# First attention of a two-layer gated network: where the second copy of each head's high half is written

## The reference

```
x = x + tanh(g_xattn[0]) * attention0(layernorm(x), ctx, ctx)
x = x + tanh(g_ffn[0])   * bit_linear_ffn(layernorm(x), ...)
x = x + tanh(g_xattn[1]) * attention1(layernorm(x), ctx, ctx, Wq, Wk, Wv)
x = x + tanh(g_ffn[1])   * experts(layernorm(x), ...)
```

```
scores = einsum('bqnd,bknd->bnqk', qh, kh) * (1 / sqrt(16))
probs  = softmax(scores, axis=-1)
out    = einsum('bnqk,bknd->bqnd', probs, vh)
```

## Time and profile before

| | |
|---|---|
| median of 3 runs | 2035.0 us (2025.68, 2035.0, 2039.9) |
| the profiled execution's own time | 2015.55 us |
| its span, first to last instruction | 2013.8 us |
| mean granted TensorE clock | 0.944 |
| first attention | from 39 to about 350 us, 64 tiles |
| busy shares of the span | PE 81%, PEld 55%, DVE 80%, ACT 59%, POOL 45% |

### The profile page before, as it was taken

The page is one execution under the profiler, slowest core; times in us unless marked ns, Lnnn a source line. Parts: engine busy times, 40 slices in busy tenths (PEclk is TensorE's granted clock), DMA queues, the critical chain, the costliest instruction groups (busy, mean ns, idle before and its releaser), DMA issues. The chain is left out here.

```text
span 2013.8 us, 53124 instructions
## 1 busy us (share of the span) xinstructions
PE 1628.2 (81%) x20058; PEld 1113.8 (55%) x20058; DVE 1620.7 (80%) x2986; ACT 1181.7 (59%) x1912; POOL 901.8 (45%) x930
## 2 busy tenths in 40 slices
PE   1899999266666666638998999997899999999998
PEld 0677777234444444426776666775455555555555
DVE  6899999558889888876887877876778778787785
ACT  1889988287776777616877777876222222222222
POOL 1455555048788778853333333332232332332322
PEclk9999999689988998869999999998899999999999
DMA  9000000100000000000002000000221211212211
GB/s 320 17 1 0 0 0 0 43 0 1 1 0 0 0 0 0 0 16 2 3 2 66 3 3 2 3 2 2 71 79 53 94 63 53 94 63 74 83 52 63
DMA packets 45435, 66.88 MB, mean 33 GB/s; under 512 B 6272, under 2 KB 36736, under 8 KB 45312
## 3 DMA queue, kind: packets, MB, share of 16 engines
q1 hardware_dynamic: 45024, 65.05, 9.7%
q10 hardware_dynamic: 288, 0.00, 0.0%
HBM read 56.39 MB, written 8.65 MB: 32 GB/s over the span
## 5 line engine op out<-in xcount | busy, mean ns | idle before, releaser
L632 ACT ACTIVATE a_exp<-a_score_t 128x1024 f32<-128x1024 f32 x256 | 262.3, 1024 | 113.4 <-PE a_score_t L442 112.6
L1514 POOL TENSOR_TENSOR e_a_parts<-e_act,e_a_parts 128x512 f16<-128x512 f32 x128 | 150.5, 1175 | 377.5 <-ACT e_a_parts L1486 377.5
L557 DVE TENSOR_REDUCE a_maxes<-a_score 128x8 f32<-128x1024 f32 x256 | 311.2, 1216 | 0.5 <-PE a_score L425 0.5
L1486 ACT ACTIVATE e_a_parts<-e_act 128x512 f16<-128x512 f32 x128 | 80.6, 629 | 343.1 <-DVE e_act L1326 343.1
L1071 POOL TENSOR_TENSOR b_hidden<-b_hidden,b_shifted 128x508 f32<-128x508 f32 x128 | 184.9, 1445 | 145.4 <-DVE b_hidden L924 145.4
L1221 PE MATMUL e_out<-e_down_t,e_a_parts 128*128 128x256 f16 x1536 | 188.9, 273 | 18.6 <-POOL e_a_parts L1514 18.6
L1207 PE MATMUL e_up_ps<-e_n_turned,e_up_t 128*128 128x512 f16 x768 | 187.1, 380 | 5.3 <-DVE e_act L1322 5.3
L1078 POOL TENSOR_TENSOR b_hidden<-b_hidden,b_scales 128x512 f32<-128x512 f32 x128 | 188.0, 1472 | 3.1 <-ACT b_scales L1053 3.1
L1207 PE MATMUL e_gate<-e_n_turned,e_gate_t 128*128 128x512 f16 x768 | 187.9, 381 | 0.2 <-issue 0.2
L1221 PEld LDWEIGHTS e_out<-e_down_t,e_a_parts 128*128 128x128 f16 x1536 | 146.6, 98 | 59.7 <-POOL e_a_parts L1514 28.9
L690 POOL TENSOR_TENSOR a_split<-ctx,a_split 128x256 f16<-128x256 f16 (+1 forms) x64 | 42.8, 669 | 305.2 <-ACT a_split L649 305.2
(11 more groups left out here) (204 smaller groups left out, 4047.3 us busy)
## 6 DMA issues: line engine op xcount, KB each, us to landing
ctx<-e_weights SPq DMA_DIRECT2D x64, 512.0 KB, 5.6
out<-x SPq DMA_DIRECT2D x16, 512.0 KB, 2.9
x<-in_x SPq DMA_DIRECT2D x3, 2048.0 KB, 16.9
ctx<-in_ctx SPq DMA_DIRECT2D x1, 4096.0 KB, 26.8
ctx<-in_ctx SPq DMA_DIRECT2D x1, 3072.0 KB, 16.4
b_raw<-in_L_ffn_w SPq DMA_DIRECT2D x2, 1024.0 KB, 7.1
x<-in_x SPq DMA_DIRECT2D x1, 1536.0 KB, 16.4
ctx<-in_ctx SPq DMA_DIRECT2D x1, 1024.0 KB, 13.4
```

Of the source, the lines that this page charges most:

```text
L557: nc.vector.tensor_reduce(maxes[:, p * PAIRS:(p + 1) * PAIRS], score[:, :].rearrange("p (h k) -> p h k", k=P), AX.X, ALU.max).then_inc(max ...
L632: nc.scalar.activation(exp32[:, u % 2, 2 * p:2 * p + 2, :], score_t[:, :].rearrange("p (g n) -> p g n", g=2), ACT.Exp, scale=DH ** -0.5 / ...
L1514: nc.gpsimd.tensor_tensor(a_parts[:, e % 2, 1, :], act3[:, e % 2, :], a_parts[:, e % 2, 0, :], ALU.subtract).then_inc(alo_ok, 1)
```

## The change

On ScalarE, L652 and L667 write the high halves once, into place 0 of each head. GpSimd gets two more instructions in each of the steps 0 to 63: behind the keys' low half a copy of place 0 to place 2, behind the queries' low half a copy of place 0 to place 1. The signals `kl_ok` and `ql_ok` move from the subtraction to the copy behind it.

```diff
-                            nc.scalar.activation(k_stack[:, u % KR, :, 0:3:2, :], twice(m.ctx[:, i, :]), ACT.Copy).then_inc(kh_ok, 1)
+                            nc.scalar.activation(k_stack[:, u % KR, :, 0, :], heads(m.ctx[:, i, :]), ACT.Copy).then_inc(kh_ok, 1)
...
-                        nc.scalar.activation(q_stack[:, u % 2, :, 0:2, :], twice(normed[:, u % 2, :]), ACT.Copy).then_inc(qh_ok, 1)
+                        nc.scalar.activation(q_stack[:, u % 2, :, 0, :], heads(normed[:, u % 2, :]), ACT.Copy).then_inc(qh_ok, 1)
...
                             nc.gpsimd.tensor_tensor(k_stack[:, u % KR, :, 1, :], heads(m.ctx[:, i, :]), k_stack[:, u % KR, :, 0, :],
-                                                    ALU.subtract).then_inc(kl_ok, 1)
+                                                    ALU.subtract)
+                            nc.gpsimd.tensor_copy(k_stack[:, u % KR, :, 2, :], k_stack[:, u % KR, :, 0, :]).then_inc(kl_ok, 1)
...
                             nc.gpsimd.tensor_tensor(q_stack[:, u % 2, :, 2, :], heads(normed[:, u % 2, :]), q_stack[:, u % 2, :, 0, :],
-                                                    ALU.subtract).then_inc(ql_ok, 1)
+                                                    ALU.subtract)
+                            nc.gpsimd.tensor_copy(q_stack[:, u % 2, :, 1, :], q_stack[:, u % 2, :, 0, :]).then_inc(ql_ok, 1)
```

## The result

| | before | with the change |
|---|---|---|
| median, 20 runs each | 2030.82 us | 2042.38 us (2036.05 to 2053.38) |
| ratio, 95% interval | | 1.0068 (1.0050 to 1.0086) |
| profiled execution, span | 2013.8 us | 2039.1 us |
| spacing of L594 in the loop | 4.82 us | 5.13 us |

A forecast was written before the change was run, and what follows sets the result against it. The first attention was taken to be bound by VectorE and TensorE waiting for each other, 4.82 us a step. L694 delaying L602, with smaller terms, adds 18.7 us to 2035.0: 2053.7 us, own range 2045 to 2062, stated range 2036 to 2090.

The forecast's parts named there:

- slower: Whole kernel: median more than 1% above the kernel before; chance 0.48.
- within 1%: Whole kernel: median within 1% (20 us) of the kernel before; chance 0.47.
- The ring: First attention: VectorE (L594 to L582, 2.88 us) and TensorE (1.94) wait for each other, 4.82 us a step; ScalarE hangs aside.
- ScalarE's 0.21 us: L652 and L667 write 256 elements, not 512: each saves 0.21 us, and L694 begins 0.10 ahead of L602.
- The collision: First attention: L694 on GpSimd holds up L602 on VectorE, 0.31 us more a step, 0.40 at the loop's turns.
- The copies: GpSimd's new copies in the first attention: 0.40 us each (0.29 to 0.67), costing nothing in the steady state.
- The sum: 64 normalisations: 15.2 us in ordinary steps, 2.8 at step 8 and loop turns, -0.3 early, +0.9 at the start; +18.7.
- The filling: Start of the first attention, where GpSimd's chain of the first tile is waited for: +0.9 us (0.6 to 1.6).
- the gain of 0.21 in each of steps 4 to 6: Steps 4 to 6 already pay 0.44 us at L602 and gain 0.21 each by the earlier L694.
- The second collision: Rival: GpSimd's queries' low half (L701) holds up L609, 0.58 us a step, in all +52 us, 2087 us; chance 0.20.
- Nothing is felt: Rival: L694 does not come ahead of L602, which keeps its 0.41 us; +1 us, 2036 us; chance 0.13.
- ScalarE's saving: Rival: ScalarE bounds the first attention, so 0.42 us saved a step gives -24 us, 2011 us; chance 0.05.

The follow-up runs named there:

- no_copies: The changed kernel without GpSimd's two copies, the places they filled set to zero once at the start; ratio to the kernel before 1.0111, spacing 5.13 us.
- keys_only: Only the keys' half of the change (L652 writes one place, GpSimd copies it) on the kernel before; ratio 1.0102, spacing 5.14 us.
- after_again: The changed kernel run once more, nothing else altered; ratio to the kernel before 1.0092, spacing 5.13 us.
- queries_only: Only the queries' half of the change (L667 writes one place, GpSimd copies it) on the kernel before; ratio 1.0042, spacing 4.82 us.
- copies_only: The kernel before, ScalarE still writing both places, with GpSimd's two copies added on top; ratio 1.0009, spacing 4.95 us.
- both_before: The kernel before, with L602 ahead of the queries' eviction and TensorE's turn of the keys ahead of the transposed scores; ratio 0.9919, spacing 4.83 us.
- before_again: The kernel before, run once more as a kernel of its own beside itself; ratio 1.0001, spacing 4.82 us.

## Why the prediction was right

**The time.** The forecast for the median was 2053.7 us, the measured median is 2042.38. Of the 11.3 us between them, 4.2 come from the start: 2035.0 was the median of three executions, and over 20 it is 2030.82. The other 7.1 are +18.7 against +11.6. The stated range took this in because it was wide, and the chances for "slower" and "within 1%" (0.48 and 0.47) decided nothing between the two. What the prediction got right is the mechanism and its price in a step.

**The ring and its two terms.** VectorE's run of 2.88 us plus TensorE's 1.94 stood as read: time taken off ScalarE was worth nothing (no_copies), time lost at L602 counted in full (keys_only), and the wait before L594 stayed at 0.25.

**ScalarE's 0.21 us.** L652 and L667 at 0.41 and 0.43 us; L694 0.10 ahead of L602, as forecast. The reading of one instruction's spacing from the second attention carried over to within a hundredth (303.12 - 302.82 = 0.30 against 0.31). The reason given for the lead being the same in every step was loose: ScalarE's exponential waits for L442 and VectorE's eviction for L472, two instructions of TensorE and not one. They stand in a fixed order with no wait between them in the trace, and the lead was 0.10 in all but the first steps and the turns of the loop.

**The collision.** L602 forecast at 0.72 and 0.80 at the loop's turns; measured 0.72, and at the turn of step 16 in the timeline:

```profile
120.76 0.67 POOL L694 TENSOR_TENSOR a_k_stack<-ctx,a_k_stack 128x256 f16<-128x256 f16 x1 [1.78 <-ACT a_k_stack L652]
120.78 0.80 DVE L602 TENSOR_SCALAR a_normed<-x,mean,rstd 128x256 f32 x1
```

**The copies.** 0.40 taken, 0.39 to 0.40 measured, hidden as forecast. The Trainium skill (GPSIMD Engine Reference, on engine selection) calls one-input work roughly line-rate and two-input work slower. The trace agrees on the order, 0.39 for the copy against 0.67 for the two-input subtraction of the same size; the prediction's estimate from the page, 0.21 plus a dispatch, fits only with 0.18 for the dispatch, which no run measures apart.

**The sum.** Forecast +18.7 (its terms add to 18.6), measured +18.3 and +18.4 in the two profiles at the first attention's end. The filling was put at 0.9 and came to 0.64 by the L594 of step 4; the gain of 0.21 in each of steps 4 to 6 came as forecast. The ratios say +14 (10 to 17) in the first comparison and +19 (12 to 26) in after_again, so the forecast lies above the interval of the first and in the middle of the second.

**The rivals.** The second collision did not come in the steady state: L609 stayed at 0.18 with L701 0.04 to 0.05 behind it. The margin was no more than that. In one step of after_again L701 is recorded 0.01 ahead, and there L609 takes 0.69, which is this rival's collision (one step of no_copies has it too, 0.68):

```profile
169.80 0.67 POOL L701 TENSOR_TENSOR a_q_stack<-a_normed,a_q_stack 128x256 f16<-128x256 f32 x1 [0.69 <-ACT a_q_stack L667]
169.81 0.69 DVE L609 TENSOR_SCALAR a_neg_max<-a_maxes 128x16 f16<-128x16 f32 x1
```

The prediction had put the distance at 0.05 rightly, but no row of before told that 0.05 was enough for L609; that part was partly luck. "Nothing is felt" is refuted by L602's 0.72, ScalarE's saving by no_copies.

**What stays open.** The difference between +18.3 net and +14 by the ratio, and the ratios of queries_only (1.0042 with no longer step), copies_only (1.0009 with 8 us of longer steps) and the faster versions (0.992 to 0.996 with 4 to 5 us, which would be 0.998). For queries_only, copies_only and both_before what the trace gives lies outside the ratio's interval, so the ratios settle little about effects this small; the traces do. The gaps are of the size of one or two 11 us steps, and those come by chance; the median of the kernel before itself differed by 11 us between comparisons (2019.46 to 2030.82), and the three rounds of experiments ran on three different chips; whether a program's place in memory makes 11 us steps likelier was not tried.

## What to carry to other kernels

Before work is shifted off an engine, ask what the engine's earlier finish releases and what that will run into: here a GpSimd instruction released 0.2 us sooner held up a VectorE instruction on the critical ring, and a kernel with less work became slower. List the pairs of VectorE and GpSimd instructions that have been seen to hold each other up, with the lead at which each wins, and compute their new distances; where the distance changes sign, hold back the one that is off the critical path. And before an edit is priced by the wait that it fills, look for the next ring: here it stood 0.015 us behind, and 0.25 us of filled wait gave almost nothing a step.

## What the runs showed of the hardware that was not expected

The place at which a collision turns is narrow, and not the recorded start alone. L602 won with L694 0.11 behind (0.40 us) and lost with it 0.02 behind (0.84). It even lost with a GpSimd instruction 0.09 behind, in an early step of before_again where GpSimd came to it straight from L694:

```profile
52.24 0.86 DVE L602 TENSOR_SCALAR a_normed<-x,mean,rstd 128x256 f32<-128x256 f32 x1
```

```profile
52.33 0.61 POOL L697 TENSOR_TENSOR a_v_pad<-ctx,a_gate 128x256 f32<-128x256 f32 x1
```

L609 won with L701 0.03 to 0.05 behind and lost with it 0.01 ahead. The Trainium skill (SBUF — State Buffer, on who interferes with whom) gives the pair to whoever issues first; these rows agree only if a GpSimd instruction's recorded start is allowed some hundredths of a microsecond of lead over that of L602 (at least 0.02, and 0.09 in the step above), and less or none over that of L609. What makes the difference was not tested.

Instructions are fetched anew at some turns of the loop, and TensorE is the engine that stands still for it. In the stretch from 199 to 245 us of the changed kernel, which begins with the first 11 us step, the instruction queue moved nine packets; from 120 us to the end of the loop the trace of before has at most one. The line of the DMA view of that stretch (packets, MB, share):

```profile
q8 instruction: 9, 0.15, 1.5%
```

A turn that does this took 5.4 to 6.0 us more than a usual one, over all traces here. At this one it is 5.9, of which 4.87 are the wait. The granted clock falls just before the wait ends: TensorE stood still from 200 us, and the clock is at its lower level (1.2 GHz) from 205 to 211 us, 0.50 in that stretch. The mean is 0.90 in the 7 us of the wait and 0.73 in the 10 us behind it, in the view by stretch:

```profile
199.00:206.00 7.00, 1.82 (x41) 1.18 (x41) 2.15 (x6) 1.66 (x3) 2.50 (x5) 0.90 0.04 7
206.00:216.00 10.00, 9.59 (x161) 7.92 (x161) 7.21 (x13) 6.26 (x9) 4.01 (x7) 0.73 0.01 2
```

The Trainium skill (Runtime: NRT & Kernel Launch, instruction fetch mechanics) says that a taken branch out of the resident window forces a fetch. The trace agrees for these turns and for the six of the second attention, each of which has a wait of 2.9 to 6.6 us (before). From 120 us on, most turns of the first attention take place with no fetch at all. It is a scatter of 6 us a time that a comparison of this kernel at a few tenths of a per cent has to live with.
